# VectorE lays the mask's bias into one score bank of every four, in the cross-attention batches

## The reference, cut to what matters

```python
logits = jnp.einsum('bhqd,bhkd->bhqk', q, k) * SCALE
mask = attn_mask[None, None, :, :]
masked = jnp.where(mask, logits, -1000000000.0)
weights = jax.nn.softmax(masked, axis=-1)
weights = weights * mask.astype(weights.dtype)
denom = jnp.maximum(weights.sum(axis=-1, keepdims=True), 1e-09)
out = jnp.einsum('bhqk,bhkd->bhqd', weights / denom, v)
```

## Time and profile before

| | us |
|---|---|
| median of 3 runs | 2356.73 (2356.29 to 2361.69) |
| the profiled execution | 2355.79 |
| its span on the core | 2353.6 |
| first exponential, last bias copy of the cross batches (L2356, L2359) | at 590.8, at 1150.0 |
| last exponential of the self batches | at 1712.9 |

### The profile page before, as it was taken

One profiled execution on the slowest core, in us unless ns is written; L12 is line 12 of the kernel. 1 busy time (PEld: TensorE's weight loads), 2 busy tenths in 40 slices (PEclk: granted clock), 3 DMA queues, 4 the chain that ended last, 5 costly groups with the idle time before them and its releaser, 6 DMA issues. The chain is left out here.

```text
span 2353.6 us, 33097 instructions
## 1 busy us (share of the span) xinstructions
PE 2143.9 (91%) x10551; PEld 1202.0 (51%) x10551; DVE 1328.7 (56%) x3625; ACT 1128.4 (48%) x2079; POOL 660.7 (28%) x671
## 2 busy tenths in 40 slices
PE   6897899994999999999999999999849999999995
PEld 2474466661333333333333444434337888888884
DVE  5556534213777777776777777787854541112125
ACT  2223311120888888888766656666612222222233
POOL 3210233333111001112124423344123333333342
PEclk9998999995999999999999999999969999999997
DMA  5335444426334332332244334344016666666684
GB/s 176 128 108 191 131 111 110 112 54 120 77 61 74 61 75 45 58 61 32 28 55 64 48 45 60 42 65 62 13 58 185 189 188 189 188 188 205 196 270 124
DMA packets 197560, 249.75 MB, mean 106 GB/s; under 512 B 26080, under 2 KB 175584, under 8 KB 195360
## 3 DMA queue, kind: packets, MB, share of 16 engines
q1 hardware_dynamic: 175808, 217.95, 36.8%
q0 software_dynamic: 20736, 29.15, 7.1%
q10 hardware_dynamic: 864, 0.79, 0.3%
HBM read 162.77 MB, written 46.52 MB: 89 GB/s over the span
## 5 line engine op out<-in xcount | busy, mean ns | idle before, releaser
L2356 ACT ACTIVATE att_prob<-att_ps 128x512 f32<-128x512 f32 x1024 | 586.5, 596 | 264.0 <-PE att_ps L2196 181.6
L2179 PE MATMUL att_pm<-att_kstack,att_qstack 96*128 96x512 bf16 x1024 | 400.3, 392 | 27.2 <-DMA att_qstack<-att_q 22.0
L2493 DVE CUSTOM_DVE_ANT_0 att_junk<-att_pm,bias 128x512 bf16<-128x512 f32 x512 | 337.0, 685 | 153.7 <-PE att_pm L2179 153.2
L2196 PE MATMUL att_ps<-att_qstack,att_kstack 99*128 99x512 bf16 x1024 | 392.1, 384 | 26.5 <-ACT att_prob L2356 10.2
L2489 DVE TENSOR_REDUCE att_tops<-att_pm 128x1 f32<-128x512 f32 x512 | 339.6, 682 | 114.8 <-PE att_pm L2179 112.8
L1591 ACT ACTIVATE exL_hid<-exL_ph,exL_b 128x256 f32<-128x256 f32 (+1 forms) x312 | 144.0, 462 | 392.4 <-PE exL_ph L1549 391.4
L1495 POOL DMA_INDIRECT sum<-exL_ys,exL_put x106 | 176.0, 1660 | 407.2 <-DVE exL_ys L1703 228.2
L1549 PE MATMUL exL_ph<-exL_xgT,exL_w 128*128 128x256 f32 (+1 forms) x1248 | 273.2, 376 | 8.8 <-issue 4.7
L2214 PE MATMUL att_po<-att_prob,att_vals 128*32 128x512 f32 x2048 | 277.0, 613 | 1.0 <-ACT att_prob L2356 1.0
L1571 PE MATMUL exL_po<-exL_w,exL_hid 128*128 128x256 f32 x1184 | 265.4, 382 | 6.0 <-ACT exL_hid L1591 4.0
L2179 PEld LDWEIGHTS att_pm<-att_kstack,att_qstack 96*128 96x128 bf16 x1024 | 100.9, 99 | 292.3 <-DVE att_tops L2493 100.4
(11 more groups left out here) (416 smaller groups left out, 2687.7 us busy)
## 6 DMA issues: line engine op xcount, KB each, us to landing
exL_w<-in_L_W SPq DMA_DIRECT2D x78, 1024.0 KB, 5.4
att_qstack<-att_q SPq DMA_DIRECT2D x186, 128.0 KB, 5.7
early_w<-in_L_W SPq DMA_DIRECT2D x16, 1024.0 KB, 5.3
att_kstack<-att_k SPq DMA_DIRECT2D x96, 128.0 KB, 4.5
att_kstack<-kstack SPq DMA_DIRECT2D x32, 256.0 KB, 5.1
kstack<-early_k SPq DMA_DIRECT2D x24, 256.0 KB, 4.3
exL_b<-in_L_b SPq DMA_DIRECT2D x39, 128.0 KB, 5.4
values<-early_vals SPq DMA_DIRECT2D x8, 574.0 KB, 3.8
```

The lines of the kernel that those rows point to most:

```text
L2179: pe.matmul(pm[i % TOPS][:], stack["q"][par][0:KR, h, t * P:(t + 1) * P], stack["k"][par][0:KR, h, :], start=True, stop=True).then_inc(s[" ...
L2196: mm = pe.matmul(ps[i % 2][:], stack["k"][par][0:KR + 3, h, kc * P:(kc + 1) * P], stack["q"][par][0:KR + 3, h, :], start=not there, stop=m ...
L2356: act.activation(prob[i % PROBS][:], ps[i % 2][:], ACT.Exp, scale=SCALE).then_inc(s["p_ready"], 1)
L2493: ins = dve.tensor_tensor_reduce(junk[:, i % TOPS, :], pm[i % TOPS][:], G["bias"][0][:, t, :], 1.0, -BIG / 2, ALU.add, ALU.max, tops[g % 2 ...
```

## The change

In the cross batches the bias of step b is no longer added by TensorE. VectorE copies it into `ps1`, with the wait that the bank is empty (all exponentials up to step d of the quad before are done), in its list directly in front of the maximum of step a. TensorE's score product of step b waits for that copy on a new semaphore, `laid_v`, and leaves out its second product. The first quad of a batch keeps the old form (`i > 1`), so that 15 of 16 quads, 120 in all, have a copy by VectorE. Self batches are untouched.

```diff
+        def laid_by_vector(of, i):
+
+            return not of.self_ and i % HG == 1 and i > 1
+
+        LAID = PER // HG - 1
...
                     there = laid(me, i)
                     if there:
                         pe.wait_ge(s["laid"], past(laid_before(me, i) + 1))
+                    if laid_by_vector(me, i):
+                        pe.wait_ge(s["laid_v"], past(me.rows * LAID + i // HG))
+                        there = True
...
+                            if laid_by_vector(w.me, g * ROUND + n + 1):
+                                dve.wait_ge(s["p_ready"], past(w.b * PER + g * ROUND + n))
+                                dve.tensor_copy(ps[1][:], G["bias"][1][:, n // HG, :]).then_inc(s["laid_v"], 1)
                             if g < 2:
                                 max_step(w.me, g + 2, n)
```

More of the change, by code:

```diff
@@ L1947, in attention @@
                  "y_stats", "y_rstd", "yn_ready", "u_ready", "u_added", "rows_stored", "shift_ready", "rexp_ready",
-                 "xn_kept", "spread", "folded", "laid", "prob_ready", "prob_stored", "flagged", "counted", "listed", "summed"]
+                 "xn_kept", "spread", "folded", "laid", "laid_v", "prob_ready", "prob_stored", "flagged", "counted", "listed", "summed"]
         s = {n: st.sem(n) for n in names}
```

## The result

The changed kernel takes 2389.11 us, the median of 4 runs (2384.76 to 2391.72), where the kernel before took 2356.51 (2355.67 to 2361.69, 4 runs). The ratio is 1.0135, interval 1.0120 to 1.0149: 32.6 us slower. The forecast was 2380, 23.2 us more, with a range from 2361 to 2391. The direction and the mechanism are those of the forecast.

A forecast was written before the change was run, and what follows sets the result against it. It took ScalarE to bound quads without jobs, TensorE having 0.11 us of slack there, and TensorE to bound quads 3 and 4. Losses and gains by quad summed to 2.90 us a batch, times eight 23.2, giving 2380, range 2361 to 2391.

The forecast's parts named there:

- the mechanism: In cross batches, score b waits for VectorE's 0.69 us copy and everything behind it comes later: quad 11 takes 0.48 us more.
- a wait is booked as one that absorbs delay: Head of quad 8: the wait for transfers of the next batch's queries soaks up 0.64 of the 0.82 us lost.

## What to carry to other kernels

An operation that takes less work off a full engine can still cost, when it puts another engine's operation and two semaphore hops into the chain that the next steps hang on. So price a move by what hangs on it and from when, and not by busy shares: here the same 0.69 us on the same engine cost 97 us one place later and 32 us in front, and gained 3 us when it filled the bank of step c, whose exponential comes later (18 us with three more edits: the copies left out where VectorE has jobs of its own, some of step b where other work hides them, the banks rotated). Before a wait is booked as one that absorbs delay, find its releaser in its own row and ask whether that releaser is fixed or moves with the chain. And where a counter modulo a number of banks starts anew in each batch, look at the seam: three banks and 64 steps cost 0.64 to 0.76 us in each batch, which an edit of an index and its wait took away. And look at the first batch by itself: a wait of 1.87 us on another engine cost it more than its length, since the clock was at the lower level behind it.

## What was not expected of the hardware

VectorE's copy of 16-bit values into a float32 bank is as long as one of float32 values out of a bank, 0.686 us for 512 columns (0.419 for 256), where its copy of 16-bit values at both ends took 0.405 for 512. ScalarE, with 0.59, is the faster of the two at this copy.

A small operation can be stretched on VectorE. L2524 over 128x16 takes 0.17 us in quad 0, and in quad 4 the same line took 1.05, while GpSimd worked over 128x512:

```profile
816.34 0.17 DVE L2524 TENSOR_TENSOR att_neg<-att_rest,att_neg 128x16 bf16<-128x16 f32 x1
```
```profile
839.21 1.16 POOL L2395 TENSOR_TENSOR att_q<-att_qf,att_q 128x512 bf16<-128x512 f32 x1
839.35 0.08 DVE L2502 DVE_READ_ACCUMULATOR2_ANT att_tops<- 128x1 f32 x1
839.35 1.05 DVE L2524 TENSOR_TENSOR att_neg<-att_rest,att_neg 128x16 bf16<-128x16 f32 x1
839.50 0.38 PE L2185 MATMUL att_pm<-att_kstack,att_qstack 96*128 96x512 bf16 x1
...
840.32 0.68 DVE L2737 CAST att_ps<-bias 128x512 f32<-128x512 bf16 x1
```

The end of L2524 (840.40) stands with the end of GpSimd's operation (840.37). It is so each time. Of the 64 executions of this line in the trace, 21 overlap a TENSOR_TENSOR of GpSimd's over 128x512. All 21 are long, 0.49 to 1.15 us, and end 0.03 behind it, while the other 43 take 0.16 to 0.18. The kernel before has 21 and 43 as well (0.48 to 0.99). VectorE's maxima over 128x512 that overlap the same operations aren't stretched: 63 of them in the cross batches of the kernel before take 0.66 to 0.69. So the one holds up the other, as far as traces can show it; no run took GpSimd's operation away, and what sets this line apart from the maxima isn't shown.
